# A two-layer gated cross-attention kernel: next period's projections among the first scores, second layer's queries beside the routing steps, layer norm steps shared with VectorE, shorter scale chains

## The reference, cut to what matters

```
x += tanh(g_xattn[0]) * attention(layernorm(x), ctx; 16 heads of 16)   # layer 0
x += tanh(g_ffn[0])   * moe(layernorm(x))      # softmax router, best 2 of 8 experts, 256 -> 256
x += tanh(g_xattn[1]) * attention(layernorm(x), ctx)                   # layer 1
x += tanh(g_ffn[1])   * ffn(layernorm(x))
# ffn: y = W2q . q(gelu(W1q . q(x)))
# q(x): scale = 127 / max(|x|, 1e-5) per token; round(x * scale) / scale
# W1q, W2q: weights rounded to -s, 0, +s with s = mean |w|
```

## Time and profile before

| what | value |
|---|---|
| median of 3 runs | 765.19 us |
| lowest and highest | 763.31, 765.99 us |
| profiled execution | 762.36 us, span 760.5 us |
| TensorE busy | 690.9 us, 91% (matmuls are pipelined, waits inside included) |
| VectorE, ScalarE, GpSimd busy | 534.3, 432.4, 164.2 us |
| granted TensorE clock | 0.973 of full |
| DMA | 66.74 MB |

### The profile page before, as it was taken

How to read it: one execution, slowest core, us unless ns; L and a number is a source line. 1 busy time by engine, 2 the same in 40 slices (tenths; PEclk the granted TensorE clock), 3 DMA queues, 4 the chain that set the end, 5 groups by cost and what they waited for, 6 DMA issues and landing times.

```text
span 760.5 us, 10162 instructions
## 1 busy us (share of the span) xinstructions
PE 690.9 (91%) x3595; PEld 331.7 (44%) x3600; DVE 534.3 (70%) x1140; ACT 432.4 (57%) x568; POOL 164.2 (22%) x300
## 2 busy tenths in 40 slices
PE   4899999899999999998999989998999899987887
PEld 2433333354544445444554445443444344332444
DVE  2577886578886687868787688865686749775334
ACT  2227666763346633665336733476776677758735
POOL 7105244630010310121101410114210301021132
PEclk9769999999999999999999999999999999999999
DMA  7749578521211501224211411126023212200000
GB/s 242 205 126 335 181 226 266 169 55 32 42 43 29 167 11 34 61 80 98 44 36 37 125 44 43 43 71 199 11 64 91 77 50 57 58 2 1 22 8 28
DMA packets 39026, 66.74 MB, mean 88 GB/s; under 512 B 5184, under 2 KB 13888, under 8 KB 38720
## 3 DMA queue, kind: packets, MB, share of 16 engines
q1 hardware_dynamic: 38128, 65.57, 30.0%
q10 hardware_dynamic: 848, 0.53, 0.2%
HBM read 38.29 MB, written 27.26 MB: 86 GB/s over the span
## 4 chain that ended last, share of the span: by engine, by line
PE 59%; DVE 14%; ACT 10%; issue 8%; POOL 8%; POOLq 0%; DVEq 0%; ACTq 0%
PE psO L799 11%; PE psS L771 8%; PE psX L724 6%; PE psT L785 6%; DVE mx L1194 6%; PE psX L860 5%; PE psX L836 4%; PE psX L861 4%; PE psX L862 4%; ACT pt L1017 3%; PE psX L744 3%; POOL parts L588 2%; DVE xs L1325 2%; ACT qf L962 2%; ACT parts L963 1%
## 5 line engine op out<-in xcount | busy, mean ns | idle before, releaser
L1017 ACT ACTIVATE pt<-psT 128x1024 f32<-128x1024 f32 x256 | 261.7, 1022 | 220.6 <-PE psT L785 218.1
L1194 DVE TENSOR_REDUCE mx<-psS 128x1 f32<-128x512 f32 x512 | 325.7, 681 | 80.5 <-PE psS L771 79.1
L771 PE MATMUL psS<-ks,qs 48*128 48x512 f32 x512 | 152.5, 514 | 15.2 <-DVE mx L1194 13.8
L799 PE MATMUL psO<-pt,vg 128*32 128x512 f32 x1024 | 139.5, 618 | 0.1
L785 PE MATMUL psT<-qs,ks 50*128 50x512 f32 x512 | 118.8, 428 | 6.9 <-ACT pt L1017 5.8
L771 PEld LDWEIGHTS psS<-ks,qs 48*128 48x128 f32 x512 | 59.9, 189 | 130.0 <-issue 73.1
L1325 DVE SCALAR_TENSOR_TENSOR xs<-psX,coef,xs 128x256 f32<-128x256 f32 x128 | 61.9, 483 | 32.4 <-PE psX L862 29.2
L588 POOL TENSOR_TENSOR parts<-qf,parts 128x512 fp32r<-128x512 f32 x30 | 38.3, 1278 | 147.2 <-ACT parts L963 147.2
L785 PEld LDWEIGHTS psT<-qs,ks 50*128 50x128 f32 x512 | 52.6, 189 | 22.4 <-ACT pt L1017 19.5
L860 PE MATMUL psX<-moeh,xh 128*128 128x512 f32 x128 | 57.4, 449 | 4.4 <-DVE xs L1325 4.4
L861 PE MATMUL psX<-moel,xh 128*128 128x512 f32 x128 | 50.7, 396 | 0.0
(11 more groups left out here) (129 smaller groups left out, 765.3 us busy)
## 6 DMA issues: line engine op xcount, KB each, us to landing
ks<-kd SPq DMA_DIRECT2D x64, 192.0 KB, 3.5
qs<-qd SPq DMA_DIRECT2D x64, 192.0 KB, 4.3
kd<-parts SPq DMA_DIRECT2D x16, 512.0 KB, 3.2
qd<-parts SPq DMA_DIRECT2D x16, 512.0 KB, 2.7
kd<-parts SPq DMA_DIRECT2D x16, 256.0 KB, 4.1
qd<-parts SPq DMA_DIRECT2D x16, 256.0 KB, 3.4
ctxb<-in_ctxT SPq DMA_DIRECT2D x7, 512.0 KB, 4.7
xs<-in_x SPq DMA_DIRECT2D x4, 512.0 KB, 6.1
```

Source lines behind the costliest of these rows:

```text
L771: mm(psS[:, i % 3, :], qs[at:at + KR, 2 * g + a, k * P:(k + 1) * P], ks[at:at + KR, 2 * g + a, :], start=True, stop=True).then_inc(pe_s, 1)
L799: i = mm(psO[32 * j:32 * j + 32, :], vg[:, p % 2, k, g * GH + j, :], pt[:, s % RING, j, :], start=k == 0, stop=k == NT - 1, tile_position= ...
L1017: a(pt[:, G % RING, 2 * half:2 * half + 2, :], psT[:], ACT.Exp, scale=SCALE).then_inc(a_exp, 1)
L1194: v.tensor_reduce(mx[:, w // GH % 2, r, col:col + 1], psS[:, i % 3, :], AX.X, ALU.max).then_inc(v_max, 1)
```

## The change: what it does

1. The query and key SPLITs of period 1 leave slots 0, 2, 4 and 6 of period 0. K's first half goes ahead of the first S, and K's second and Q's two halves go into the lead, among the S products (slots 22, 25, 28). The second XT of that layer norm goes behind the first S.
2. The key SPLITs of period 3 go from slots 0 and 2 of period 1 to its slots 16 and 18. In periods 1 to 4 the two VV steps go from slots 11 and 15 to slots 6 and 10.
3. In periods 2, 3 and 4 the layer-1 LNN, XT and query SPLITs go from slots 3 to 10 to slots 13 to 18, among the router's steps; period 5 keeps them.
4. In periods 5 to 7 the first XB goes from slot 14 to slot 15, before the second.
5. For sequence 0 and in the tail, the eight GpSimd steps of LNC become one on VectorE (LNE), the power on GpSimd, and five on VectorE (LND).
6. The tail is put in another order, and 18 of its 46 BUSY products go.
7. XQ and HQ have four VectorE steps in place of five, and the scale that GpSimd waits for is the third of them.

```diff
+    put(lead, 20, ("XT", (1,)))
     put(lead, 21, ("RELOAD", (0, 2)))
-    put(lead, 22, ("RELOAD", (0, 3)))
+    put(lead, 22, ("RELOAD", (0, 3)), ("SPLIT", ("K", 1, 1)))
+    put(lead, 25, ("SPLIT", ("Q", 1, 0)))
+    put(lead, 28, ("SPLIT", ("Q", 1, 1)))
...
-                put(p, 11, ("VV", (p + 1, 0)))
-                put(p, 15, ("VV", (p + 1, 1)))
+                put(p, 6, ("VV", (p + 1, 0)))
+                put(p, 10, ("VV", (p + 1, 1)))
...
+            if two:
+                put(p, 13, ("LNN", (1, p - 2, 0, 2)))
+                put(p, 14, ("LNN", (1, p - 2, 2, 4)))
+                pair(p, 15, "XT", step=0)
+                pair(p, 16, "SPLIT", "Q", B + p - 2, step=2)
...
-            put(p, 14, ("XB", (0, 1, 0, NT)))
-            put(p, 15, ("XB", (1, 2, 0, NT)))
+            put(p, 15, ("XB", (0, 1, 0, NT)), ("XB", (1, 2, 0, NT)))
...
-    put(NP, 4, ("OP", (1, b, 0)), ("ST", (b, 0)), ("ST", (b, 1)), ("LNC", (b, 0, 2)), ("LNN", (b, 0, 2)))
-    put(NP, 4, ("OP", (1, b, 1)), ("ST", (b, 2)), ("ST", (b, 3)), ("LNC", (b, 2, 4)))
-    put(NP, 4, ("BUSY", (29,)))
-    put(NP, 5, ("XQ", (0, 2)), ("LNN", (b, 2, 4)), ("XB", (0, NC, 0, 2)), ("BUSY", (4,)), ("XQ", (2, 4)))
-    put(NP, 5, ("F1", (0,)), ("XB", (0, NC, 2, 4)), ("BUSY", (4,)), ("F1", (1,)), ("F1", (2,)), ("F1", (3,)),
-        ("BUSY", (9,)))
+    put(NP, 4, ("OP", (1, b, 0)), ("ST", (b, 0)), ("ST", (b, 1)), ("LNE", (b, 0, 2)), ("OP", (1, b, 1)))
+    put(NP, 4, ("LND", (b, 0, 2)), ("LNN", (0, b, 0, 2)), ("ST", (b, 2)), ("ST", (b, 3)))
+    put(NP, 4, ("LNE", (b, 2, 4)), ("LND", (b, 2, 4)))
+    put(NP, 4, ("BUSY", (20,)))
+    put(NP, 5, ("XQ", (0, 2)), ("LNN", (0, b, 2, 4)), ("XB", (0, NC, 0, 2)), ("BUSY", (4,)), ("F1", (0,)))
+    put(NP, 5, ("XQ", (2, 4)), ("XB", (0, NC, 2, 4)), ("BUSY", (4,)), ("F1", (1,)), ("F1", (2,)), ("F1", (3,)))
...
-        if kind in ("LNC", "LNN", "XQ"):
-            n.n[kind + " tiles"] = n.n.get(kind + " tiles", 0) + args[-1] - args[-2]
+        if kind in ("LNC", "LND", "LNN", "XQ"):
+            tiles = ("LNC" if kind == "LND" else kind) + " tiles"
+            n.n[tiles] = n.n.get(tiles, 0) + args[-1] - args[-2]
...
-                if due(a_xn, n("LNC tiles") - 2 * NT):
-                    pool.wait_ge(a_xn, n("LNC tiles") - 2 * NT)
+                if due(a_xn, n("LNN tiles")):
+                    pool.wait_ge(a_xn, n("LNN tiles"))
...
+            def power(b, t0, t1):
+                i = n("LNC tiles") // NT % 2
+                if due(c_pool, POOL_HALFS):
+                    pool.wait_ge(c_pool, POOL_HALFS)
+                if due(v_ln, n("LNE", LND_OPS, 1)):
+                    pool.wait_ge(v_ln, n("LNE", LND_OPS, 1))
+                g.tensor_tensor(lnw[:, i, 0, t0:t1], lnw[:, i, 5, t0:t1], halfs[:, t0:t1], ALU.pow).then_inc(p_pow, 1)
...
-            def ln(b, t0, t1):
-                i = n("LNN tiles") // NT + 1
+            def ln(swap, b, t0, t1):
+                i = n("LNN tiles") // NT + 1 + swap
                 if due(p_ln, n("LNC", LN_OPS)):
                     act.wait_ge(p_ln, n("LNC", LN_OPS))
+                if due(v_ln, n("LND", LND_OPS)):
+                    act.wait_ge(v_ln, n("LND", LND_OPS))
...
+                if due(v_xq, n("XQ", XQ_OPS)):
+                    act.wait_ge(v_xq, n("XQ", XQ_OPS))
...
+            def variances(b, t0, t1):
+                i = n("LNC tiles") // NT % 2
+                if due(v_st, 2 * (n("LNC tiles") + t1 - t0)):
+                    dve.wait_ge(v_st, 2 * (n("LNC tiles") + t1 - t0))
+                if due(a_xn, n("LNN tiles")):
+                    dve.wait_ge(a_xn, n("LNN tiles"))
+                v.tensor_scalar(lnw[:, i, 5, t0:t1], mv[:, i, t0:t1, 1], LN_EPS, None, ALU.add).then_inc(v_ln, 1)
+
+            def coefficients(b, t0, t1):
+                i = n("LNC tiles") // NT % 2
+                k = n("LND", LND_OPS)
+                mean = mv[:, i, t0:t1, 0]
+                r0, t, _, r1, nb, ve = (lnw[:, i, q, t0:t1] for q in range(6))
+                if due(p_pow, n("LND") + 1):
+                    dve.wait_ge(p_pow, n("LND") + 1)
+                if due(v_ln, k + 1):
+                    dve.wait_ge(v_ln, k + 1)
+                v.tensor_tensor(t, r0, r0, ALU.mult).then_inc(v_ln, 1)
+                if due(v_ln, k + 2):
+                    dve.wait_ge(v_ln, k + 2)
+                v.tensor_tensor(t, t, ve, ALU.mult).then_inc(v_ln, 1)
+                if due(v_ln, k + 3):
+                    dve.wait_ge(v_ln, k + 3)
+                v.tensor_scalar(t, t, -0.5, 1.5, ALU.mult, ALU.add).then_inc(v_ln, 1)
+                if due(v_ln, k + 4):
+                    dve.wait_ge(v_ln, k + 4)
+                v.tensor_tensor(r1, r0, t, ALU.mult).then_inc(v_ln, 1)
+                if due(v_ln, k + 5):
+                    dve.wait_ge(v_ln, k + 5)
+                v.scalar_tensor_tensor(out=nb, in0=mean, scalar=-1.0, in1=r1, op0=ALU.mult, op1=ALU.mult
+                                       ).then_inc(v_ln, 1)
...
-                v.tensor_scalar(dqf[:, 0:1], wmean[:, 0:1], 1.0 / 127.0, None, ALU.mult).then_inc(v_scale, 1)
-                v.tensor_scalar(dqf[:, 1:2], wmean[:, 1:2], gt[:, 3:4], 1.0 / 127.0, ALU.mult, ALU.mult
-                                ).then_inc(v_scale, 1)
+                v.tensor_copy(dqf[:, 0:1], wmean[:, 0:1]).then_inc(v_scale, 1)
+                v.tensor_scalar(dqf[:, 1:2], wmean[:, 1:2], gt[:, 3:4], None, ALU.mult).then_inc(v_scale, 1)
...
-                v.tensor_scalar(top, top, Q_EPS, None, ALU.max).then_inc(v_xq, 1)
+                v.tensor_scalar(top, top, Q_EPS, 1.0 / 127.0, ALU.max, ALU.mult).then_inc(v_xq, 1)
                 if due(v_xq, i + 2):
                     dve.wait_ge(v_xq, i + 2)
+                v.reciprocal(inv, top).then_inc(v_xq, 1)
                 v.tensor_scalar(deq, top, dqf[:, 0:1], None, ALU.mult).then_inc(v_xq, 1)
-                v.reciprocal(inv, top).then_inc(v_xq, 1)
-                if due(v_xq, i + 4):
-                    dve.wait_ge(v_xq, i + 4)
-                v.tensor_scalar(inv, inv, 127.0, None, ALU.mult).then_inc(v_xq, 1)
...
-                v.tensor_scalar(big, big, Q_EPS, None, ALU.max).then_inc(v_hq, 1)
+                v.tensor_scalar(big, big, Q_EPS, 1.0 / 127.0, ALU.max, ALU.mult).then_inc(v_hq, 1)
                 if due(v_hq, i + 2):
                     dve.wait_ge(v_hq, i + 2)
+                v.reciprocal(inv, big).then_inc(v_hq, 1)
                 v.tensor_scalar(deq, big, dqf[:, 1:2], None, ALU.mult).then_inc(v_hq, 1)
-                v.reciprocal(inv, big).then_inc(v_hq, 1)
-                if due(v_hq, i + 4):
-                    dve.wait_ge(v_hq, i + 4)
-                v.tensor_scalar(inv, inv, 127.0, None, ALU.mult).then_inc(v_hq, 1)
```

59 lines of the change are left out of this document (33 added, 26 removed).

## The result

The changed kernel took 766.89 us (median of 12 executions, 764.61 to 772.90), the kernel before 764.21 (12 executions on the same chip, 761.01 to 765.99). The ratio is 1.0048 with a 95% interval of [1.0027, 1.0069]: half a per cent slower, where 752 had been forecast. The profiled execution took 764.70 us with a span of 762.9; before it was 760.5. So the spans differ by +2.4 us where the sum said -13.2.

The account below looks back on a forecast made before the run. TensorE was taken to set the pace, its stalls being lost time. Terms -5.1 - 1.0 - 3.3 - 2.5 - 2.6 + 1.3 = -13.2 us took the profiled execution from 762.36 to 749.2, 752 on the median; range 746 to 760.

Parts of the forecast that it names:

- Term +1.3: Tail: later XQ, fewer BUSY products ahead of HT, and +1.5 for half clock; sum +1.3 us, bounds -0.5 and +3.5.
- The term for periods 2 to 4: Moved queries and VV: -0.6 - 1.9 + 0.3 + 1.1 = -1.1 us a period, -3.3 for three; bounds -8 and +4.
- Its parts as written: Period 1: SPLITs leave and return, VV moves, a stall fills, slot 17's clock, exposed layer norm; sum stated -2.5 us.
- Rival D: Slots 13 to 19: ScalarE becomes the bound, periods 2 to 4 each 4.2 us longer, 768 us; chance 0.04.
- Rival C: Periods 1 to 4: stalls only move (+5.5), and the tail pays fully for the clock (+2); 760 us; chance 0.17.
- 0.6 was the price: Period 7: later XB delays F1's input by one ScalarE pass, a loss of 0.6 us.
- -6.1: Periods 5 to 7: XB into slot 15 -5.1 us and shorter XQ and HQ -1.0 us.
- rival B: Start: the lead is free, stores don't hold the maxima's transfer, T(0) near 48, 748 us; chance 0.13.
- the bound that the forecast named: Start: stores find room and VectorE holds T(0) near 48, -6.5 us at T(8).
- The term -2.6: Start: T(0) to T(8) 8.1 us shorter, T(0) 5.5 later behind queued stores; -2.6 at T(8).
- the 0.05 for slower: Whole kernel: chance given to a slower result, from rival D and what is unforeseen; faster had 0.92.

Follow-up runs that it names:

- the first experiment: Changed kernel with the second half's XQ(2,4) ahead of F1(0) in the tail's table; 762.71 us, ratio 0.9981 to the kernel before.
- the kernel with eight added products: Mended tail, shorter chains, XB in 15 (14 in period 7), periods 1 to 4 changed, old start; eight unused products in each of periods 2 to 4; 757.01 us, ratio 0.9904.
- the one execution at full clock: Mended tail, shorter chains, old start, periods 1 to 4 changed, but second VV in slot 11 in periods 2 to 4; 756.98 us, ratio 0.9935; period 1 took 86.8.
- the last kernel: As the kernel with eight added products, but four unused products a period, in periods 1 to 4; 752.36 us, ratio 0.9850 to the kernel before.

## Why the prediction was wrong

- **Tail, the step that failed outright.** The forecast followed XQ(0,2) behind the second half's layer norm and found its 1 us, but did not follow XQ(2,4), which the same edit put behind F1(0). Term +1.3, measured +5.8; the order alone is 4.6 of it (shown by the first experiment), and the half clock behind 20 BUSY products, which the forecast put at +1.5, is 3.0 with the wait and 1.6 without it (39.7 against 38.1, the latter without the changed start as well).
- **Periods 1 to 4, the step where the size was off.** The term for periods 2 to 4 counted slots at full clock and had no price for the clock. At full clock its sum holds. Slots 3 to 8 are 0.6 us shorter, as forecast; T(9) to T(13) is 10.1, as forecast; T(15) to T(19) is 14.3 in the kernel with eight added products (2.69 + 2.78 + 3.25 + 5.55), forecast 14.2; together periods 2 to 4 would be 0.9 to 1.2 shorter each (estimates, from the kernels with four and eight products), forecast 1.1. A part of that is luck: slot 18 kept a stall that was to go (0.82 us, for VectorE's `xs`) and takes 5.55 where 4.7 was worked out, and slots 15 and 16 are shorter than forecast by as much. What the term measured in the changed kernel was +4.0 in place of -3.3, and the kernels with added products show the clock as the cause. The new layout makes slots 11 to 14 thin, with a wait of 0.68 us ahead of an XT and short ones for VectorE's and GpSimd's steps (0.54 and 0.52), where before no wait in slots 9 to 15 was above 0.12, and half clock begins there or just behind, in slots 12 to 16. The Trainium skill ("TensorE: Matmul & The Clock Gate", A second HAM failure mode: psum-queue depth-cycling) tells of an engine that idles for moments between groups of matmuls, often enough for the clock to swing; the trace agrees: no gap in slots 9 to 15 is above 0.7 us, and the clock falls.
- **Period 1.** Its parts as written (-3.3 + 3.8 - 1.9 - 1.4 - 0.4 + 1.2) come to -2.0, not to -2.5, so the whole sum should have read -12.7. It measured 0.0 at a clock of 0.96, and -2.5 in the one execution at full clock. That this meets the -2.5 is chance: 1.85 of it is slot 17, for which the forecast counted 0.4.
- **Rival D**, ScalarE as the bound, fell: the periods with added products have the same ScalarE passes (46.2 us busy) and are shorter. Rival C was nearest in its price for the middle, but by another mechanism.
- **XB in slot 15.** Right in the slots (T(14) to T(16) 4.4 us, forecast 4.6). Off in what surrounds them: in period 5 half clock now falls on the SPLIT of slot 12 (3.56 us in place of 1.9), and period 7 lost 2.4 where 0.6 was the price, at a clock of 0.91, before 0.98. The sum of periods 5 to 7 was -2.9 for -6.1.
- **Start.** The profiled execution has T(0) at 48.25, not 52: that was rival B's sign, but not its reason. The stores did fill the queue (DMA share above 1.0 until 46 us) and did hold the small transfer: issued at 41.6, its 32 packets of 512 B were moved between 46.8 and 47.4 us. But T(0) was not waiting for it: S products, which VectorE's maxima let go one by one, stand right ahead, and T(0) starts together with the last of them. It did so in all seven kernels with the changed start, and in the kernel before too (46.52). So the bound that the forecast named, T(0) held by VectorE near 48, came although no room was found. And what VectorE waits for is TensorE's own work, three SPLITs between the first scores of the lead, behind which VectorE stood idle for 1.1, 1.1 and 3.6 us:

```profile
30.55 1.98 PE L745 MATMUL psX<-ctxb,wk 128*128 128x512 f32 x4
...
35.37 1.98 PE L745 MATMUL psX<-xnt,wq 128*128 128x512 f32 x4
...
41.13 3.23 PE L745 MATMUL psX<-xnt,wq 128*128 128x512 f32 x4
...
48.25 1.15 PE L806 MATMUL psT<-qs,ks 50*128 50x512 f32 x2
```

  With the changed start T(0) lay at 47.8 to 51.6 us in seven kernels, with the old one at 42.9 to 44.2 in the eleven experiments that had it, and period 1 began at 126.9 to 131.6 and at 127.9 to 130.3. The -4.4 of the profiled execution was luck on both sides: its 126.89 is the earliest of its seven, and the 131.28 of the kernel before, like its T(0) at 46.52, is later than in any of the eleven. The term -2.6 should have been near 0 or above; with the start on top of a base the ratio was 0.3 and 0.5% higher.
- **A row misread.** The prediction has the clock at 5 and 6 tenths in slices 2 and 3 and at 9 in a few later ones. The row has 7 and 6, and 9, its highest digit, in all others, so it can't tell 0.90 from 1.00. Nothing in the sum rests on it.
- **The sum once more.** What a microsecond at half clock costs can be read in two ways: 1.4 us for the stretch in period 2 of the last kernel, whose clock of 0.98 is 0.02 x 2 x 90 = 3.6 us at half, so 0.4; and a straight line through times and clocks of the twelve executions of the changed kernel, which gives 0.33. At these prices 28 us more at half clock are 9 to 11 us (estimates). The 28 are a net sum: some 18 more in periods 2 to 4, 10 more in period 7, 10 more in the tail, and less at the start. With the 4.6 of the order, -13.2 becomes +0.6 to +2.4, of which 1.5 are counted twice, since the forecast had them for the tail's clock. The measured +2.4 is met to within about 3 us and not better.

The range (746 to 760) and the 0.05 for slower were too sure in the same place: most of the terms leaned on one assumption, that the clock would stay as it was, so they could not miss independently.

## What to carry to other kernels

A sum of slots at full clock is only half a forecast: ask of each slot that an edit makes thinner whether TensorE keeps its clock there, and give that a term and a rival of its own. When work is moved and the clock falls, a few products that nobody needs, put into waits, can be worth more than the move: here four of 256 columns a period took the moved layout from a ratio of 0.992 to 0.985 (with XB of period 7 moved back as well). After reordering a table, follow every entry whose wait counts "all so far", not only the one that the edit is about.

## What the runs showed of the hardware

- Half clock came here without a long idle time. In slots 9 to 15 of periods 2 to 4 of the changed kernel TensorE had no gap above 0.7 us, and half clock came in slots 12 to 16 of each; with eight products put among its waits it came in none of six such periods.
- Most of one kernel's scatter goes with its clock: the changed kernel's executions run from 764.6 us at a mean clock of 0.960 to 772.9 at 0.945. Not all of it: with eight added products they stay within 2.4 us, at clocks of 0.975 to 0.977 that do not order them.
- Of a microsecond at half clock 0.3 to 0.4 us was lost here, not half, by the two readings above. That other engines' waits cover the rest is argued, not shown.
- A transfer of 8 KB issued behind 2.4 MB of stores had its packets moved 5 us after its issue (41.6, and 46.8 to 47.4 us), and cost nothing, since its consumer was held until 48.25 by something else.
